# Moving a state-space scan and a router out of an attention loop, and making half of its decays on another engine

## What is computed

```
x += attention of 16 heads over 2048 context keys, causal          (t=0, "first attention")
x += selective state-space scan:  z = LN(x) @ Wx; dt = softplus(z)
       h[n] = exp(-dt * exp(A_log[n])) * h[n] + dt * B[n] * x;  y = sum_n h[n] * C[n] + D * x,  n < 16     (t=1)
x += x @ W + bias + top-2 of 16 rank-16 experts, chosen by a router (t=2, "router and low-rank part")
x += masked attention of one head over the 2048 keys               (t=3)
x += attention of 16 heads, local and compressed, with q,k,v projections of 256 x 2048 each  (t=4)
x += top-2 of 8 experts of three layers with gelu                  (t=5)
```

## Time and profile before

| | |
|---|---|
| median of 3 runs | 515.19 us |
| the profiled execution | 514.26 us, span 512.0 us from first to last instruction |
| TensorE clock granted, mean | 0.936 of full |
| busy: PE / DVE / ACT / POOL | 425.1 / 345.8 / 269.4 / 121.7 us |
| chain that ended last | PE 58%, DVE 23%, ACT 8%, issue 6% |

### The profile page before, as it was taken

The page is one execution under the profiler, slowest core; times in us unless marked ns, Lnnn a source line. Parts: engine busy times, 40 slices in busy tenths (PEclk is TensorE's granted clock), DMA queues, the critical chain, the costliest instruction groups (busy, mean ns, idle before and its releaser), DMA issues.

```text
span 512.0 us, 8986 instructions
## 1 busy us (share of the span) xinstructions
PE 425.1 (83%) x3584; PEld 311.0 (61%) x3584; DVE 345.8 (68%) x544; ACT 269.4 (53%) x579; POOL 121.7 (24%) x78
## 2 busy tenths in 40 slices
PE   0269889988875985694989998997789799999997
PEld 0116556656553773534843473445679699999996
DVE  3797667676569935699565565684562589778772
ACT  4305697766585452540322442457784076777762
POOL 3010545000274000280003235250300213333300
PEclk9999899998797798678999999999799979999999
DMA  6598176652511082000920000005800197540000
GB/s 217 141 291 214 28 187 166 165 133 52 150 48 32 3 299 68 25 0 1 397 97 1 1 0 3 0 0 193 300 1 2 43 360 246 173 165 1 2 2 20
DMA packets 24329, 54.11 MB, mean 106 GB/s; under 512 B 5113, under 2 KB 13529, under 8 KB 20954
## 3 DMA queue, kind: packets, MB, share of 16 engines
q1 hardware_dynamic: 24288, 53.54, 33.4%
HBM read 40.65 MB, written 0.26 MB: 80 GB/s over the span
## 4 chain that ended last, share of the span: by engine, by line
PE 58%; DVE 23%; ACT 8%; issue 6%; DMA 2%; POOL 2%; SPq 0%; ACTq 0%; DVEq 0%; POOLq 0%
PE ps L1268 17%; PE ps L1089 8%; PE ps L902 5%; PE ps L889 4%; PE ps L858 4%; DVE mx L1647 4%; DVE reg_b L1439 3%; DVE reg_a L1439 2%; ACT reg_b L665 2%; PE ps L1233 2%; PE ps L1223 2%; PE ps L1222 2%; PE ps L997 2%; PE ps L1016 1%; DVE reg_b L1430 1%
## 5 line engine op out<-in xcount | busy, mean ns | idle before, releaser
L1647 DVE TENSOR_REDUCE mx<-ps 128x1 f32<-128x1024 f32 x64 | 77.0, 1221 | 40.4 <-PE ps L858 28.3
L665 ACT ACTIVATE reg_b<-ps 128x512 f32<-128x512 f32 x128 | 75.4, 599 | 39.9 <-PE ps L889 20.8
L889 PE MATMUL ps<-qreg,reg_b 98*128 98x128 bf16 x512 | 51.0, 235 | 6.1 <-ACT reg_b L665 4.7
L889 PEld LDWEIGHTS ps<-qreg,reg_b 98*128 98x128 bf16 x512 | 38.3, 106 | 18.6 <-ACT reg_b L665 8.8
L1268 PE MATMUL ps<-part_a 128*128 128x256 f32 x384 | 48.2, 283 | 0.4 <-DVE part_a L1792 0.4
L386 POOL TENSOR_TENSOR rstd<-ve,cf 128x1 f32<-128x1 f32 x12 | 6.8, 563 | 172.3 <-DVE ve L1341 172.3
L858 PE MATMUL ps<-reg_b,qreg 96*128 96x512 bf16 x96 | 36.3, 448 | 13.7 <-DMA reg_b<-reg_b 7.6
L1089 PE MATMUL ps<-reg_b,xT 128*128 128x512 f32 x96 | 47.6, 618 | 0.0
L1268 PEld LDWEIGHTS ps<-part_a 128*128 128x128 f32 x384 | 46.9, 192 | 0.6 <-DVE part_a L1792 0.6
L902 PE MATMUL ps<-reg_b 128*32 128x128 f32 x1024 | 45.9, 299 | 0.0
L800 ACT ACTIVATE reg_a<-ps,b 128x256 f32<-128x256 f32 x64 | 30.2, 472 | 24.0 <-PE ps L1268 24.0
(11 more groups left out here) (279 smaller groups left out, 869.8 us busy)
## 6 DMA issues: line engine op xcount, KB each, us to landing
reg_b<-in_w SPq DMA_DIRECT2D x16, 512.0 KB, 7.1
reg_b<-in_w SPq DMA_DIRECT2D x8, 1024.0 KB, 7.0
reg_b<-reg_b SPq DMA_DIRECT2D x56, 128.0 KB, 3.7
reg_b<-in_w_qkv SPq DMA_DIRECT2D x3, 2048.0 KB, 13.4
reg_b<-reg_a SPq DMA_DIRECT2D x40, 128.0 KB, 3.6
reg_a<-in_ctxK SPq DMA_DIRECT2D x4, 1024.0 KB, 6.9
reg_a<-in_ctx SPq DMA_DIRECT2D x8, 512.0 KB, 5.1
reg_a<-in_ctxT SPq DMA_DIRECT2D x2, 2048.0 KB, 9.7
```

Of the source, the lines that this page charges most:

```text
L665: sc.activation(pT[n % 3], score_b[n % 2], ACT.Exp).then_inc(S("exp_done"), 1)
L889: mm = pe.matmul(cols, kS[g % 3][0:SROWS, c // 8, j, P * (c % 8):P * (c % 8 + 1)], qT[b][0:SROWS, HPG * hg + j, :], start=not last, stop=True)
L1647: ve.reduce_max(mx[:, piece // 2, piece % 2:piece % 2 + 1], score_a[m % 2].rearrange("p i k -> p (i k)"), X_AXIS).then_inc(S("max_done"), 1)
```

## The change

1. The scans and reads of sequence 0 go from places in the loop's DVE list to behind the last maximum (`masked_weight(1)`, then two scans, then two reads). The decays' exponentials on ACT are cut in two (1024 elements each) and spread over groups 6 and 7.
2. `sum_states(0, *)`, the transpose for t=2 and the router's products leave PE's loop and stand behind it. Four of the 16 spreads go from group 6 to group 7.
3. For sequence 1 DVE's `decay_exponent` is gone. ACT makes each of the 2 x 16 decays from the step sizes directly, `exp(scale * dt)` with the state's rate as the scale of each partition, 128 x 128 elements each; the rates are now stored negated. POOL's `state_input` for sequence 1 goes to DVE.
4. The order behind the loop is new on PE, ACT and DVE: the router of sequence 1 (`lora_products(1)`, `lora_logits(1)` and so on) goes between the quarters of the first projections, `sum_states(1, *)` goes behind `outputs3(0)`, `max3(0)` ahead of the reads.
5. The three parts of `w_qkv` change places, and the first is loaded at `m3_done` 1. The nine bias rows go ahead of the weights, to other partitions.

```diff
-SPREAD_AT = [(5, c) for c in range(8, 15)] + [(6, c) for c in (0, 1, *range(4, 11))]
+SPREAD_AT = [(5, c) for c in range(8, 15)] + [(6, c) for c in (0, 1, 4, 8, 10)] + [(7, c) for c in range(4, 8)]
...
 SP
-            sp.wait_ge(S("hc_done"), KD * NB)
-            for j in range(3):
-                if j == 2:
-                    sp.wait_ge(S("y_ps"), 2)
-                load(w_qkv[:, j, :, :], ...)
-            sp.wait_ge(S("x_done0"), 4)
             sp.wait_ge(S("b48_split"), 1)
             for j in range(3):
                 for t in range(3):
...
+            for j, (name, count) in enumerate((("m3_done", 1), ("hc_done", KD * NB), ("y_ps", 2))):
+                sp.wait_ge(S(name), count)
+                load(w_qkv[j], io["w_qkv"][j].rearrange("(k p) n -> p k n", p=P), f"wqkv_in{j}")
...
 POOL, behind the loop
-            inv_sqrt(2, 0)
-            inv_sqrt(1, 1)
-            inv_sqrt(3, 0)
-            state_input(1, 0)
-            state_input(1, 1)
-            inv_sqrt(2, 1)
-            inv_sqrt(4, 0)
+            inv_sqrt(1, 1)
+            inv_sqrt(2, 0)
+            inv_sqrt(3, 0)
+            inv_sqrt(4, 0)
+            inv_sqrt(2, 1)
             inv_sqrt(3, 1)
...
 ACT
+            def decay_exp(h, half):
+                sc.wait_ge(S("dta_done"), h + 1)
+                part = decay[0][:, h, 8 * half:8 * half + 8]
+                sc.activation(part, part, ACT.Exp).then_inc(S("decay_done"), 1)
+            def decay_by_state(h, states):
+                sc.wait_ge(S("dtx_done"), NB)
+                for n in states:
+                    sc.activation(decay[1][:, h, n, :], dt[1][:, P * h:P * (h + 1)], ACT.Exp, scale=ea[:, h, n:n + 1])\
+                        .then_inc(S("decay_done"), 1)
...
-                      ... (6, 2): [(decay_exp, 0, 0)], (6, 6): [(decay_exp, 0, 1)],
-                      (7, 11): [(transposed_x, 2, 0)], (7, 13): [(hidden_exp, 0)]}
+                      ... (6, 4): [(decay_exp, 0, 0)], (6, 7): [(decay_exp, 0, 1)], (7, 1): [(decay_exp, 1, 0)],
+                      (7, 3): [(decay_exp, 1, 1)], (7, 9): [(weigh_masked, 1)]}
...
-            weigh_masked(1)
-            gap_exp(0)
             transposed_x(1, 1)
-            wxaT(0)
             copy_z(1)
             softplus_exp(1)
+            transposed_x(2, 0)
+            hidden_exp(0)
             softplus_log(1)
-            for i in range(8):
+            exp_table()
+            gap_exp(0)
+            decay_by_state(0, range(0, 8))
+            wxaT(0)
+            for i in range(4):
                 bc_copy(1, i)
             transposed_x(3, 0)
-            decay_exp(1, 0)
-            decay_exp(1, 1)
+            decay_by_state(0, range(8, NS))
+            for i in range(4, 6):
+                bc_copy(1, i)
+            decay_by_state(1, range(0, NS))
+            for i in range(6, 8):
+                bc_copy(1, i)
             exp3(0)
...
 PE
-                      (7, 0): [(sum_states, 0, 0)], (7, 4): [(sum_states, 0, 1)], (7, 9): [(x_to_columns, 2, 0)],
-                      (7, 11): [(lora_products, 0)], (7, 15): [(lora_logits, 0)]}
+                      (7, 4): [(misc_read, "o_all", 7)]}
...
+            sum_states(0, 0)
+            sum_states(0, 1)
             x_to_columns(1, 1)
+            step_sizes(1)
+            x_to_columns(2, 0)
+            lora_products(0)
+            state_maps(1)
+            lora_logits(0)
             lora_columns(0)
-            step_sizes(1)
             lora_up(0)
-            state_maps(1)
-            for i in range(8):
+            for i in range(4):
                 spread(1, i)
             x_to_columns(3, 0)
             scores3(0, 0)
+            for i in range(4, 6):
+                spread(1, i)
             scores3(0, 1)
-            sum_states(1, 0)
-            sum_states(1, 1)
+            for i in range(6, 8):
+                spread(1, i)
             p3_to_columns(0)
             outputs3(0)
-            x_to_columns(2, 1)
-            lora_products(1)
+            sum_states(1, 0)
             x_to_columns(4, 0)
             block_scores(0)
-            lora_logits(1)
-            projection(0, 0, range(0, 2))
-            lora_columns(1)
-            block_column(0)
-            lora_up(1)
-            projection(0, 0, range(2, 4))
-            block_entries(0)
+            sum_states(1, 1)
+            projection(0, 0, range(0, 2))
+            x_to_columns(2, 1)
+            projection(0, 0, range(2, 3))
+            lora_products(1)
+            projection(0, 0, range(3, 4))
+            block_column(0)
+            projection(0, 1, range(0, 1))
+            lora_logits(1)
+            projection(0, 1, range(1, 2))
+            lora_columns(1)
+            block_entries(0)
+            projection(0, 1, range(2, 3))
+            lora_up(1)
+            compressed(0)
+            projection(0, 1, range(3, 4))
             x_to_columns(3, 1)
             scores3(1, 0)
-            compressed(0)
             scores3(1, 1)
-            projection(0, 1)
             pe.wait_ge(S("cms_done"), 1)
             rotated_to_columns(0, 0)
...
 DVE, behind the loop (in the loop: scan(0, 0) at (7, 3) and read_states(0, 0) at (7, 6) are gone)
             masked_weight(1)
+            scan(0, 0)
             scan(0, 1)
+            read_states(0, 0)
             read_states(0, 1)
+            normalise(1)
+            ln_stats(1, 1)
+            add_inputs(0)
+            ln_apply(1, 1)
             key_mask()
             add_states(0)
...
+            step_magnitude(1)
             lora_hidden(0)
+            step_and_input(1)
             lora_top(0)
-            normalise(1)
-            ln_stats(1, 1)
-            ln_apply(1, 1)
             lora_weighted(0)
-            step_magnitude(1)
             split_maps(1)
             lora_add(0)
             ln_stats(3, 0)
-            step_and_input(1)
+            bias_parts()
             ln_apply(3, 0)
-            decay_exponent(1, 0)
-            decay_exponent(1, 1)
+            state_input(0)
             scan(1, 0)
+            state_input(1)
+            scan(1, 1)
+            max3(0)
             read_states(1, 0)
-            scan(1, 1)
             read_states(1, 1)
-            max3(0)
+            add_inputs(1)
             tables()
+            add3(0)
...
             rope_q(0)
             max3(1)
             compressed(0)
```

More of the change, by code:

```diff
@@ L109, in perceiver_program @@
         roped = reg_b[:, 16384:18432].rearrange("p (h d) -> p h d", h=NH)
-        bias3 = view(reg_b, 20480, 1024, BF16)
+        bias3 = view(reg_b, 12544, 1024, BF16)
         squares = reg_b[:, 14336:16384].rearrange("p (h d) -> p h d", h=NH)
@@ L408, in late_part3, with state_input @@
                     .then_inc(S("k3_done"), 1)
[L410 to L415, removed]
+            def state_input(h):
+                pool.wait_ge(S("dtx_done"), 1)
+                pool.wait_ge(S("bc_sb"), 8)
+                pool.tensor_tensor(state[0][:, h], tmp[0][:, h * P:(h + 1) * P].unsqueeze(1).to_broadcast([P, NS, P]),
+                                   bc_row[0][:, 0:NS, :], ALU.mult).then_inc(S("dbx_done"), 1)
             def decay_exponent(h):
@@ L596, in bc_copy, with exp_table @@
                     .then_inc(S("bc_sb"), 1)
-            def decay_exp(b, h):
-                sc.wait_ge(S("dta_done"), KD * b + h + 1)
-                sc.activation(decay[b][:, h], decay[b][:, h], ACT.Exp, scale=-1.0).then_inc(S("decay_done"), 1)
+            def decay_exp(h, half):
[7 more added lines that the diff above has]
+                        .then_inc(S("decay_done"), 1)
+            def exp_table():
+                sc.activation(small[1][:, 7:8], neg_half, ACT.Exp)
             def hidden_exp(b):
@@ L1425, in split_maps, with state_input @@
                 last.then_inc(S("bc_split"), 1)
[L1427 to L1432 removed]
+            def state_input(h):
+                ve.wait_ge(S("dtx_done"), NB)
+                ve.wait_ge(S("bc_sb"), 20)
+                ve.tensor_tensor(state[1][:, h], tmp[1][:, h * P:(h + 1) * P].unsqueeze(1).to_broadcast([P, NS, P]),
+                                 bc_row[1][:, 0:NS, :], ALU.mult).then_inc(S("dbx_done"), 1)
             def scan(b, h):
[L1436 removed]
+                ve.wait_ge(S("decay_done"), 2 * (h + 1) if b == 0 else 2 * KD + NS * (h + 1))
                 link(ve.memset(decay[b][:, h, :, 0:1], 0.0))
@@ L1521, in add3, with bias_parts @@
                     .then_inc(S(f"x_done{b}"), 1)
-            def tables():
+            def bias_parts():
                 ve.wait_ge(S("tab_in"), 224)
@@ L1531, in tables @@
                     .then_inc(S("b48_split"), 1)
+            def tables():
                 for name, c, s, rows in (("q", cos2, sin2, P), ("k", cos2, sin2, P), ("e", cose, sine, NC)):
@@ L1634, in _ @@
             beside = {(0, 7): [(ln_stats, 0, 1)], (0, 8): [(ln_apply, 0, 1), (split_queries, 1)], (3, 8): [(masked_weight, 0)], (5, 2): [(normalise, 0)], (5, 3): [(ln_stats, 1, 0)],
```

(26 more changed lines are left out.)

53 lines of the change are left out of this document (25 added, 28 removed).

## The result

| | before | changed |
|---|---|---|
| median of 20 runs each | 513.03 us | 516.25 us |
| ratio, 95% interval | | 1.0072, 1.0049 to 1.0095 |
| the profiled execution (span) | 514.26 (512.0) | 515.66 (513.7) |
| TensorE clock granted, mean | 0.936 | 0.934 |

509.3 was forecast, with a range of 502 to 514.5. 516.25 lies above it, and a loss of 3.2 us stands where a gain of 5.9 was forecast.

The account below looks back on a forecast made before the run. Bound by DVE's scan waits from 150 to 262 us, then by PE's projections until about 350. Gain 15.6 from the loop, less 0.9, 3.6, 3.7 and 1.5, is 5.9: 508.4 profiled, 509.3 median, range 502 to 514.5.

Parts of the forecast that it names:

- Group 6, 17.1: Loop group 6 without scan, read and PE's wait: group 3's 14.8 plus 1.25 spreads and 1.0 half exponentials, 17.1 us.
- Group 7, 18.0: Loop group 7: 24.3 less 7.4 state sums and 2.5 router, plus spreads, half exponentials and waits, 18.0 us.
- rival C: Group 7 runs at half clock, PE waiting on ACT; 5 us slower than before, 520; chance 0.11.
- Loop to first projection, 65.0: From the loop's end at 182 to the first projection at 247.0, before 197.6 and 261.7.
- The sixteen small exponentials at 0.30: ACT's exponentials for sequence 1's second half, 0.30 us each, 4.8 us together, bounds 1.9 to 7.5.
- the table load without a gap: Ahead of sequence 1's logarithm: 1.28 us, next instruction right behind; the skill's 1.38 us drain not added.
- `scores3` at half clock: PE's scores3(0, 0) behind the loop, after short steps with waits: 2.0 us added for low clock, bounds 0 to 3.
- First projection to the rotated transposes, +7.3: Between first projection and rotated transposes: 3.6 us more router work on PE, and a new 3.7 us wait.
- The wait on `cms_done`: PE stands still 3.7 us ahead of rotated_to_columns(0, 0) while DVE does max3(1) and four steps of compressed.
- Clock behind it, 1.5: PE's low clock after the cms_done standstill costs 1.5 us, bounds 0 to 3.
- A: Rival: no low clock ahead of scores3 or behind the stall, small exponentials 0.2; gain 11, so 504; chance 0.15.
- B: Rival: ACT's small exponentials take 0.47 each and clock costs 0.5 more; gain 1.3, so 513.9; chance 0.14.

Follow-up runs that it names:

- the edit that took it away: The order put back, plus compressed(0) ahead of max3(1), last quarter of projection(0, 1) behind scores3(1, 1), rotated columns ahead of exp3(1): 504.50 us, ratio 0.9857.
- the order put back: The changed kernel with split_maps(0) at (6, 2) and step_and_input(0) at (6, 3) again, nothing else: 504.93 us, ratio 0.9852.

## Why the prediction was wrong

**The step that failed** is the one at which the sum starts. "I follow a schedule by milestones" begins with group 6: what lies ahead of it was taken as unchanged, so the exchange of `split_maps(0)` and `step_and_input(0)` at (6, 2) and (6, 3) got neither a term nor a rival. (Places in DVE's list run ahead of the group that PE is in: these lie in group 5.) It cost 31.21 - 24.53 = 6.7 us in group 5 and 18.30 - 15.44 = 2.9 in group 6, where PE comes in at half clock: 9.5 us against a forecast gain of 5.9. The profiled executions with and without the exchange differ by 10.8 us in all. Another 2.2 of it lie in group 4, at a clock of 0.83 instead of 0.91. That isn't tied to the exchange: the kernel before with the exchange has 17.98 there, and kernels without it have 16.7 to 18.7. Why this execution has 20.2 stays open.

The prediction had the rule in hand: a scan "stands still meanwhile" while POOL is at work beside it. It then asked only where the scans meet POOL ("that the scans still meet POOL is excluded"), not which other DVE instruction meets it, nor what releases POOL. The one step that POOL's exponents wait for was moved ahead, and the next DVE step is the one on which PE waits.

The Trainium skill has the rule, and the prediction didn't draw on it: "SBUF — State Buffer", in Who interferes with whom, says that `copy`, `cast` and `tensor_scalar` can enter two-port modes and then contend with GpSimd, as does a DVE instruction with two SBUF inputs against one that reads SBUF, and that whoever issues first has the shared ports for the whole instruction. The traces agree in each case: cast from SBUF to SBUF 3.2 instead of 0.22, scan 8.6 and `m<-mx` 1.94 with two SBUF inputs instead of 4.42 and 0.16, cast from PSUM 0.29 and difference with one SBUF input 0.30 beside POOL. Each of those that stood still was issued after POOL's product had begun.

**Group 6, 17.1:** 16.0 measured, and 15.44 from maxima to maxima when group 5 is in order. The forecast put 2.3 us on the five spreads and two half exponentials; over group 3's 14.8 these are 0.6 to 1.2.

**Group 7, 18.0:** 16.7. The clock is 1.00; rival C (half clock there) didn't come.

**Loop to first projection, 65.0:** 66.6 in the changed kernel (188.6 to 255.25). The sixteen small exponentials at 0.30, the scan that waits on ACT (3.5), the table load without a gap, `scores3` at half clock: each as assumed. From the loop's end to the fourth spread's copy it took 24.9 where the sum has 24.4, though 4.2 of the 16.1 us between 190.3 and 206.4 have no number of their own there (`step_magnitude`, the logarithm, `step_and_input`). What is over is mostly the 1.3 us of low clock behind PE's wait of 9.95, for which there is no term. The experiments add that the small exponentials' price was the wrong question: they wait for spread 4 on PE, and the variant with large ones is as fast.

**First projection to the rotated transposes, +7.3:** +6.8. The wait on `cms_done` was forecast to 0.1 us. That it costs 3.7 in the end is not shown: the edit that took it away put 2.64 one step later, most of it by its own order.

**Clock behind it, 1.5:** the last stretch is 1.4 us longer in the changed kernel and 1.1 with the order put back.

**Rivals.** A and B had the sizes of terms for their subject; C had a low clock in the loop, but in group 7, where 1.00 was granted. The time above 514.5 came from a mechanism that none of them held. The bound of a gain of 3 to 9 us is 512.2 by the prediction's own 515.2, not 512.5, which changes nothing. With the order put back each stretch comes out within 1.1 us of its forecast (group 6 0.8 better, the stretch to the first projection 1.0 worse), so the agreement does not rest on the total alone. That kernel takes 504.93 us where the sum says 509.3; 2.0 of the 4.4 us is the kernel before, which took 513.2 beside it and 515.19 in the three runs on which the number was built.

## What to carry to other kernels

Where a diff exchanges two steps of an engine, ask of each which other engine it releases and what then runs beside the step that follows; an earlier start of POOL can be a loss. Look for DVE instructions that take and give SBUF alone next to POOL's long products, however small. Here casts, scans and a maximum of 128 x 4 stood still until the POOL instruction that was running had ended, and where PE waited for them its clock fell too. Start the sum at the first line of the diff, not at the first one that looks important.

## What the runs showed of the hardware

- A cast of 32 x 128 from SBUF to SBUF lasted 0.22 us alone and 2.20, 3.21 and 3.28 beside POOL's products of 3.59, each time until 0.1 us after the product that was running. From PSUM it lasted 0.28 to 0.29 beside POOL; the cast of 96 x 128 from PSUM lasted 0.28 beside POOL (with the two steps exchanged) and 0.29 without (before). Keeping a residual in PSUM costs 0.07 us for each cast, and POOL did not hold it up.
- A `TENSOR_TENSOR` of 128 x 4 with both inputs in SBUF took 1.94 us beside POOL's product and 0.16 without.
- POOL's own product was not slowed by the casts: 7.17 us for two, as before. Nor by a scan: the two inputs took 8.97 together beside it, and 4.55 each elsewhere, while the scan took 8.65 instead of 4.42.
- After PE stood still for 7.27 us, its clock was at the lower level (values at 1.08 for 0.65) from 144.3 to about 157. The loss in the two groups, 9.5 us, is more than the standstill itself, though 1.8 us of another standstill are gone in the same stretch.
- `ACT_TABLE_LOAD` took 1.28 us with the next activation right behind it, twice within 3 us.
